# Two-layer kernel (cross attention, then a top-2 expert MLP): the gathered rows are transposed by SyncE's transposing DMAs instead of TensorE and ScalarE's copy

## The chip, the cores and the metric

One core of one Trainium2 chip. The metric is the device time of one launch in microseconds (us). The kernel before takes 813.24 us, the median of 3 runs (811.27 to 814.58). Its profiled execution is a run of its own and took 818.82 us; the span of its trace is 817.0 us.

## The reference, cut to what matters

`x` and `ctx` are 64 batches of 128 rows of 256 numbers, all float32.

```
# layer 1: x = x + xattn(layernorm(x), ctx, ctx)
score = softmax(einsum('bci,bcj->bij', ctx, q) / 16, axis=0)     # softmax over the 64 batches
out   = einsum('bci,bij->bcj', ctx, score)
# layer 2: x = x + moe(layernorm(x)); 8192 tokens of 256, 8 experts, hidden 512, top 2
logits = x @ router_w.T ; topk = top_k(logits, 2) ; probs = softmax(topk)
hmid   = gelu(x @ w1[e].T + b1[e])            # 256 -> 512, per chosen expert
y      = hmid @ w2[e].T + b2[e]               # 512 -> 256
out    = sum over the two chosen experts of probs * y
```

## The kernel before, in words

The first three stages read `ctx` and `x` three times: scores and their maximum over the batches, exponentials and their sum, and then attention with the routing logits (`attend`). They end near 300 us of the span. `attend` leaves for each token one row in a DRAM table (`rows_first`), 514 words wide: the layer's result x2 (256 float32 words), the normalised row as a high and a low float16 half, that is 512 float16 numbers in the next 256 words (from `XN`), and the two probabilities. Short routing work then sorts the tokens by expert: for each of two rounds (first choice, second choice) 39 groups of 256 tokens, each group owned by one expert. That makes `ALL` = 78 groups.

The expert stage runs from 331 us to the end, one group a step, as a software pipeline written out by hand: in each step every engine runs the parts of `group` in the order of its source, each part for another group, `L_...` steps after the group's gather.

- GpSimd (POOL), L517 to L532: in step g it issues the two indirect DMAs that gather the 256 rows of group g into two of the 12 row buffers (6 lanes of two, L506), then waits until the group of 4 steps ago is summed (`x_sum`) and issues the two indirect DMAs that scatter it (L513), to `rows_second` in round one, to the output in round two. Between the rounds, for 4 groups, x2 is gathered once more from `rows_second` (`late_loads`) after the scatters of round one have landed.
- TensorE, L661 to L695: the first product of group g-3 (24 matmuls of 256 columns, L670), then the transposes of group g-2 (8 of 128x128 float16 into PSUM bank 0, L681), then the second product of group g-4 (24 matmuls of 256 columns, L693). The wait of the first product for the transposed rows is L664, the wait of the transposes for the gathered rows is L676, and L677 holds them until the bank is copied out.
- ScalarE, L1044 to L1059: four Gelus of group g-3 (L1051), then the copy of the transposed rows of group g-2 from PSUM to `xT`, one of two buffers in SBUF (L1059).
- VectorE, L935 to L960: splits the Gelu's result in a high and a low float16 half (L942, L944), adds the bias (L931), and adds probability times product to the row (L958), which raises `x_sum`.
- SyncE (SP) has nothing to do in this stage: its last transfer, `b2` at L434, is issued before the routing.

The row buffers are read by the transposes and freed by the landing of the scatter (`x_out`, six semaphores, one a lane). A late gather overwrites the row buffer that the transposes read, so it waits for them (L525).

Of the kernel before, what the change touches and what calls it, by code (L numbers as in the profile page):

```python
# [26 lines left out]
F16 = mybir.dt.float16  # L27
# [3 lines left out]
ACT = mybir.ActivationFunctionType  # L31
AX_X = mybir.AxisListType.X

P = 128
BATCH, ROWS, DIM = 64, 128, 256
EXPERTS, HID = 8, 512
TOKENS = BATCH * ROWS
HC = DIM // P
FC = HID // P
GROUP = 256  # L40
SUB = GROUP // P
# [8 lines left out]
XN = DIM  # L50
# [4 lines left out]
PAIRS = BATCH // 2  # L55
RING = 4
LANES = 6
L_TR, L_G1, L_G2 = 2, 3, 4


def pipeline(eng, count, unroll, peel, last_lag, body):
# [41 lines left out]
def live(i, k, lag, count):  # L103

    return not isinstance(i, int) or 0 <= i + k - lag < count


def after(eng, sem, count):

    if not isinstance(count, int) or count > 0:  # L110
        eng.wait_ge(sem, count)
# [21 lines left out]
def xattn_ffn(nc, x, ctx, router_w, w1, b1, w2, b2, out):  # L133
# [7 lines left out]
    with ExitStack() as stack:  # L141
        def sb(name, shape, dt=F32):
            return stack.enter_context(nc.sbuf_tensor(name, shape, dt))

        def sem(name):
            return stack.enter_context(nc.semaphore(name))

        def sems(name, n):
            return [sem(f"{name}{i}") for i in range(n)]
# [4 lines left out]
        w1T = [sb(f"w1T_{p}", [P, FC, HC, EXPERTS * P], F16) for p in ("high", "low")]  # L154
# [15 lines left out]
        ident16 = sb("ident16", [P, P], F16)  # L170
# [22 lines left out]
        psum = stack.enter_context(nc.psum_tensor("psum", [P, 8, 512], F32))  # L193
# [63 lines left out]
        a_logit = sem("a_logit")  # L257
# [29 lines left out]
        def take(words, rows=P):  # L287
            taken[0] += words
            return slots[0:rows, taken[0] - words:taken[0]]
# [33 lines left out]
        row_buf = [take(ROW) for _ in range(LANES * SUB)]  # L323
# [2 lines left out]

        flat = work[:].rearrange("p a b -> p (a b)")
        act32 = [flat[:, j * FC * GROUP:(j + 1) * FC * GROUP] for j in range(2)]
        xT = [flat[:, 2 * FC * GROUP + j * 512:2 * FC * GROUP + (j + 1) * 512].bitcast(F16) for j in range(2)]


        x_rows_in = sems("x_rows_in", LANES)
        x_late_in = sems("x_late_in", L_G2)
        x_out = sems("x_out", LANES)
        x_tr = sem("x_tr")
        x_xT = sem("x_xT")
        x_hid = sem("x_hid")
        x_act = sem("x_act")
        x_high = sem("x_high")
# [4 lines left out]
        ALL = ROUNDS * GROUPS  # L344
# [11 lines left out]
        def late_loads(step):  # L356

            first = step - L_G2 + (step > GROUPS + L_G2)
            return [g for g in range(first, step - L_G2 + 2) if is_late(g) and step >= GROUPS + L_G2]
# [74 lines left out]
            sp.dma_start(b2_all, b2.rearrange("e (o h) -> o (e h)", o=1).to_broadcast([P, EXPERTS * DIM])).then_inc(r_b2, 16)  # L434


        @block.gpsimd
        def _(pool):
            pool.memset(ident[:], 0.0).then_inc(s_zero, 1)
# [63 lines left out]
            def gather(sources, g, signal):  # L503

                for s in range(SUB):
                    pool.indirect_dma_start(row_buf[g % LANES * SUB + s], None, sources,  # L506
                                            bass.IndirectOffsetOnAxis(ap=index[:, g * 4 + s:g * 4 + s + 1], axis=0)).then_inc(signal, 16)
# [9 lines left out]
            for step in range(ALL + L_G2):  # L517
                if step == GROUPS:
                    pool.wait_ge(r_index, 2)
                if step == GROUPS + L_G2:  # L520
                    for r in range(LANES):
                        pool.wait_ge(x_out[r], 32 * len(range(r, GROUPS, LANES)))
                for g in late_loads(step):
                    pool.wait_ge(x_rows_in[g % LANES], 32 * len(range(g % LANES, g + 1, LANES)))
                    pool.wait_ge(x_tr, g + 1)  # L525
                    gather(table[1], g, x_late_in[g - GROUPS])
                if step < ALL:
                    after(pool, x_out[step % LANES], step // LANES * 32)
                    gather(table[0] if step < GROUPS or is_late(step) else table[1], step, x_rows_in[step % LANES])
                if step >= L_G2:  # L530
                    pool.wait_ge(x_sum, step - L_G2 + 1)
                    scatter(step - L_G2)  # L532
# [5 lines left out]
        def _(pe):  # L538
            pe.wait_ge(s_const, 1)
            pe.wait_ge(s_rw_in, 16)  # L540
            for h in range(HC):
                mm = pe.transpose(psum[:, 6, h * 8:h * 8 + 8], rw_in[:, h * P:(h + 1) * P], ident[0:8, 0:8])
            pe.wait_ge(s_b1_in, 16)
            for f in range(FC):
                mm = pe.transpose(psum[:, 7, f * 8:f * 8 + 8], work[0:EXPERTS, 16 + f // 2, (f % 2) * P:(f % 2 + 1) * P], ident[0:8, 0:8])
# [87 lines left out]
            for r in range(ROUNDS):  # L633

                pe.matmul(psum[:, r, :], before[:], onehot[:, r * 512:(r + 1) * 512], start=True, stop=False)
                for e in range(EXPERTS):
                    mm = pe.matmul(psum[0:BATCH, 2, r * 8 + e:r * 8 + e + 1], hot[:, r, :, e], ones16[:, 0:1], start=True, stop=True)
# [21 lines left out]

            def group(i, k, n, rnd):  # L660
                if live(i, k, L_G1, ALL):  # L661
                    g, r2 = i + k - L_G1, (k - L_G1) % 2
                    e = pe.value_load(owner_i[0:1, bass.ds(g, 1)], min_val=0, max_val=EXPERTS - 1)
                    pe.wait_ge(x_xT, g + 1)  # L664
                    after(pe, x_act, g * 2 - 2)
                    for f in range(FC):
                        h = psum[:, 2 + 2 * r2 + f // 2, (f % 2) * GROUP:(f % 2 + 1) * GROUP]
                        for c in range(HC):
                            for px, pw in ((0, 0), (1, 0), (0, 1)):
                                mm = pe.matmul(h, w1T[pw][:, f, c, bass.ds(e * P, P)], xT[r2][:, (px * HC + c) * GROUP:(px * HC + c + 1) * GROUP],  # L670
                                               start=(c == 0 and px == 0 and pw == 0), stop=(c == HC - 1 and pw == 1))
                        if f % 2:
                            mm.then_inc(x_hid, 1)
                if live(i, k, L_TR, ALL):
                    g, r = i + k - L_TR, (k - L_TR) % LANES
                    pe.wait_ge(x_rows_in[r], n * 32 + (k - L_TR) // LANES * 32 + 32)  # L676
                    after(pe, x_xT, g)  # L677
                    bank = psum[:, 0, :].bitcast(F16)
                    for c in range(2 * HC):
                        for s in range(SUB):  # L680
                            mm = pe.transpose(bank[:, (c * SUB + s) * P:(c * SUB + s + 1) * P],  # L681
                                              row_buf[r * SUB + s][:, XN:XN + DIM].bitcast(F16)[:, c * P:(c + 1) * P], ident16[:])
                    mm.then_inc(x_tr, 1)
                if live(i, k, L_G2, ALL):
                    g, r2 = i + k - L_G2, (k - L_G2) % 2
                    e = pe.value_load(owner_i[0:1, bass.ds(g, 1)], min_val=0, max_val=EXPERTS - 1)
                    pe.wait_ge(x_low, g * 2 + 2)
                    after(pe, x_sum, g - 1)
                    for s in range(SUB):
                        y = psum[:, 6 + r2, s * DIM:(s + 1) * DIM]  # L690
                        for f in range(FC):
                            for pa, pw in ((0, 0), (1, 0), (0, 1)):
                                mm = pe.matmul(y, act16[r2][pa][:, f * GROUP + s * P:f * GROUP + (s + 1) * P],  # L693
                                               w2T[pw][:, f, bass.ds(e * DIM, DIM)], start=(f == 0 and pa == 0 and pw == 0), stop=(f == FC - 1 and pw == 1))
                    mm.then_inc(x_y, 1)  # L695
                if is_step(i, k, LIST_STEP):
                    list_tokens(1)
# [278 lines left out]
        def _(act):  # L976
# [66 lines left out]
            def group(i, k, n, rnd):  # L1043
                if live(i, k, L_G1, ALL):  # L1044
                    g, r, r2 = i + k - L_G1, (k - L_G1) % LANES, (k - L_G1) % 2
                    e = act.value_load(owner_i[0:1, bass.ds(g, 1)], min_val=0, max_val=EXPERTS - 1)
                    after(act, x_low, g * 2 - 2)
                    for f in range(FC):
                        if f % 2 == 0:
                            act.wait_ge(x_hid, g * 2 + f // 2 + 1)  # L1050
                        last = act.activation(act32[r2][:, f * GROUP:(f + 1) * GROUP], psum[:, 2 + 2 * r2 + f // 2, (f % 2) * GROUP:(f % 2 + 1) * GROUP],  # L1051
                                              ACT.Gelu, bias=b1_rows[:, bass.ds(e * FC + f, 1)], scale=1.0 / WSCALE)
                        if f % 2:
                            last.then_inc(x_act, 1)
                if live(i, k, L_TR, ALL):
                    g, r2 = i + k - L_TR, (k - L_TR) % 2
                    act.wait_ge(x_tr, g + 1)
                    after(act, x_hid, g * 2 - 2)
                    act.activation(xT[r2], psum[:, 0, :].bitcast(F16), ACT.Copy).then_inc(x_xT, 1)  # L1059
            expert_steps(act, group)  # L1060


# [17 lines left out]
```

## Time and profile before

| what | value |
|---|---|
| median of 3 runs | 813.24 us |
| profiled execution, and the span of its trace | 818.82 us, 817.0 us |
| first gather of the expert stage issued at | 331.2 us of the span |
| first and last transposes on TensorE | 336.8 and 797.6 us |
| matmuls of the first and of the second product | 1872 and 1872 |
| transposes, their busy time | 624, 48.2 us |
| ScalarE's copies, their busy time | 78, 79.9 us |
| GpSimd's indirect DMAs | 164 gathers, 156 scatters |
| granted TensorE clock, mean of the span | 0.943 |

The table says how much there is of each kind. The matmul records are pipelined: one of 276 ns starts every 109 ns. So a step's length is read from the starts, and the share of the span that a kind of work costs from where it stands on the chain that ends last, not from its busy time. Times below are us from the start of the span unless said otherwise; clock 1.00 is the 2.4 GHz level.

### The profile page before, as it was taken

Reading aid. Unit: us, or ns where it says so; the run is one execution under the profiler, and the core shown is the slowest. Engines: PE = TensorE matmul, PEld = TensorE weight load, DVE = VectorE, ACT = ScalarE, POOL = GpSimd, SP = SyncE. Lnnn points to the kernel's source line nnn. Section 1 sums busy time; section 2 is a strip of 40 time slices with the busy share of each in tenths; the row PEclk is TensorE's granted clock in tenths of the full one; section 3 lists DMA queues with packets and bytes.
Section 4 is the critical chain, followed back from the end, with each engine's and each line's share of the span. In section 5 each row is a group of like instructions: output and inputs, shape, how many; then the busy total and the mean of one; then the engine's idle time right before and its main releaser. Section 6 shows DMA issues by size and latency. Waiting matters only on the chain. (4 is left out here: it accounts for less than half of the span.)

```text
span 817.0 us, 22178 instructions
## 1 busy us (share of the span) xinstructions
PE 742.1 (91%) x5931; PEld 647.5 (79%) x5932; DVE 618.5 (76%) x1520; ACT 387.1 (47%) x716; POOL 538.5 (66%) x658
## 2 busy tenths in 40 slices
PE   6999999598999844499999999999979999999995
PEld 4777888477788734399999999999958999999995
DVE  5998999897999967786667676627467766767664
ACT  3554666375766751144444445414424444444441
POOL 4664777586888720657777777736677777777764
PEclk9999999798999955599999999979999999999998
DMA  7887876256888650445555555534355444444440
GB/s 217 259 258 233 242 234 203 88 172 207 268 270 270 228 199 0 103 141 159 183 163 186 167 181 179 160 114 132 104 167 143 152 146 134 132 139 130 139 113 1
DMA packets 82201, 137.20 MB, mean 168 GB/s; under 512 B 10075, under 2 KB 55140, under 8 KB 82032
## 3 DMA queue, kind: packets, MB, share of 16 engines
q0 software_dynamic: 23104, 68.43, 28.0%
q1 hardware_dynamic: 59056, 68.26, 26.8%
q8 instruction: 22, 0.36, 0.2%
q14 instruction: 19, 0.16, 0.1%
HBM read 94.56 MB, written 47.59 MB: 174 GB/s over the span
## 5 line engine op out<-in xcount | busy, mean ns | idle before, releaser
L1051 ACT ACTIVATE work<-psum,b1T 128x256 f32<-128x256 f32 x312 | 131.0, 471 | 259.3 <-PE psum L670 259.2
L670 PE MATMUL psum<-work,w1T_high 128*128 128x256 f16 x1248 | 213.1, 276 | 2.7 <-ACT work L1059 2.7
L693 PE MATMUL psum<-w2T_high,slots 128*128 x1248 | 210.2, 274 | 1.1 <-issue 1.1
L670 PE MATMUL psum<-work,w1T_low 128*128 128x256 f16 x624 | 172.3, 276 | 0.0
L693 PE MATMUL psum<-w2T_low,slots 128*128 x624 | 170.8, 274 | 0.0
L942 DVE CAST slots<-work 128x512 f16<-128x512 f32 x156 | 68.8, 441 | 118.6 <-ACT work L1051 118.4
L670 PEld LDWEIGHTS psum<-work,w1T_high 128*128 x1248 | 123.4, 99 | 18.7 <-issue 3.1
L693 PEld LDWEIGHTS psum<-w2T_high,slots 128*128 128x128 f16 x1248 | 119.2, 98 | 14.8 <-issue 1.8
L551 PE MATMUL psum<-slots,work 128*128 (+1 forms) x512 | 124.2, 393 | 7.1 <-ACT slots L981 6.5
L506 POOL DMA_INDIRECT slots<-rows_first,slots x86 | 89.4, 1039 | 60.5 <-DVE slots L903 34.6
L513 POOL DMA_INDIRECT rows_second<-slots x78 | 83.4, 1069 | 55.9 <-issue 34.7
L551 PEld LDWEIGHTS psum<-slots,work 128*128 128x128 f32 x512 | 94.6, 193 | 31.8 <-issue 14.9
L944 DVE TENSOR_TENSOR slots<-work,slots 128x512 f16<-128x512 f32 x156 | 108.5, 696 | 5.4
L513 POOL DMA_INDIRECT out_x<-slots x78 | 81.9, 1050 | 42.4 <-issue 32.4
L1059 ACT ACTIVATE work<-psum 128x1024 f16<-128x1024 f16 x78 | 79.9, 1024 | 33.5 <-PE psum L681 33.5
L506 POOL DMA_INDIRECT slots<-rows_second,slots x78 | 77.5, 994 | 25.5 <-issue 25.2
L931 DVE SCALAR_TENSOR_TENSOR slots<-slots 128x256 f32<-128x256 f32 x156 | 68.7, 482 | 28.1 <-issue 13.9
L623 PE MATMUL psum<-slots,work 128*128 (+1 forms) x256 | 66.5, 404 | 4.4 <-DVE slots L822 4.3
L958 DVE SCALAR_TENSOR_TENSOR slots<-psum,slots 128x256 f32<-128x256 f32 x156 | 68.2, 479 | 2.8 <-PE psum L693 2.5
L670 PEld LDWEIGHTS psum<-work,w1T_low 128*128 x624 | 61.8, 99 | 7.9
L693 PEld LDWEIGHTS psum<-w2T_low,slots 128*128 128x128 f16 x624 | 61.3, 98 | 7.3
L478 POOL TENSOR_TENSOR smax<-slots,smax 128x768 f32<-128x768 f32 x31 | 52.3, 1686 | 19.1 <-ACT slots L988 17.4
(123 smaller groups left out, 1076.9 us busy)
## 6 DMA issues: line engine op xcount, KB each, us to landing
work<-in_ctx SPq DMA_DIRECT2D x96, 256.0 KB, 3.6
rows_first<-slots SPq DMA_DIRECT2D x32, 514.0 KB, 3.9
slots<-in_x SPq DMA_DIRECT2D x32, 256.0 KB, 3.8
work<-in_L_ffn_w SPq DMA_DIRECT2D x32, 256.0 KB, 3.2
work<-in_x SPq DMA_DIRECT2D x32, 256.0 KB, 3.1
slots<-rows_first,slots POOLq DMA_INDIRECT x86
rows_second<-slots POOLq DMA_INDIRECT x78
slots<-rows_second,slots POOLq DMA_INDIRECT x78, 3.7
```

The source lines that it names most:

```text
L506: pool.indirect_dma_start(row_buf[g % LANES * SUB + s], None, sources, bass.IndirectOffsetOnAxis(ap=index[:, g * 4 + s:g * 4 + s + 1], axi ...
L513: pool.indirect_dma_start(table[1] if g < GROUPS else out_rows, bass.IndirectOffsetOnAxis(ap=index[:, g * 4 + 2 + s:g * 4 + 3 + s], axis=0 ...
L551: mm = pe.matmul(psum[:, r2, h * DIM:(h + 1) * DIM], ctx_ring[:, place, h * P:(h + 1) * P], slot(b, 0, DIM), start=True, stop=True)
L623: mm = pe.matmul(psum[:, 2 + r, j * DIM:(j + 1) * DIM], a_ctxT[:, 2 * r + j, h * P:(h + 1) * P], slot(m * 2 + j, h * DIM, DIM), start=(h = ...
L670: mm = pe.matmul(h, w1T[pw][:, f, c, bass.ds(e * P, P)], xT[r2][:, (px * HC + c) * GROUP:(px * HC + c + 1) * GROUP], start=(c == 0 and px ...
L693: mm = pe.matmul(y, act16[r2][pa][:, f * GROUP + s * P:f * GROUP + (s + 1) * P], w2T[pw][:, f, bass.ds(e * DIM, DIM)], start=(f == 0 and p ...
L931: last = dve.scalar_tensor_tensor(rows[:, X2:X2 + DIM], b2_all[:, bass.ds(e * DIM, DIM)], rows[:, PR + now:PR + now + 1], rows[:, X2:X2 + ...
L942: dve.tensor_copy(act16[r2][0][:, cols], act32[r2][:, cols]).then_inc(x_high, 1)
L944: dve.tensor_tensor(act16[r2][1][:, cols], act32[r2][:, cols], act16[r2][0][:, cols], ALU.subtract).then_inc(x_low, 1)
L958: last = dve.scalar_tensor_tensor(rows[:, X2:X2 + DIM], psum[:, 6 + r2, s * DIM:(s + 1) * DIM], rows[:, PR + now:PR + now + 1], rows[:, X2 ...
L1051: last = act.activation(act32[r2][:, f * GROUP:(f + 1) * GROUP], psum[:, 2 + 2 * r2 + f // 2, (f % 2) * GROUP:(f % 2 + 1) * GROUP], ACT.Ge ...
L1059: act.activation(xT[r2], psum[:, 0, :].bitcast(F16), ACT.Copy).then_inc(x_xT, 1)
```

## The change

The eight TensorE transposes of a group and ScalarE's copy are removed. In their place SyncE issues, for each group, two transposing DMAs from SBUF to SBUF, one for each row buffer: 128 partitions x 512 float16 numbers in, `[128, 4, 128]` out. `xT` gets a third buffer. The first product waits for 32 counts on its buffer's semaphore; SyncE waits for the gathered rows and for the first product of three groups ago, which is the last reader of the buffer. The late gather waits on the DMAs' semaphore instead of on TensorE's. The lags of the other parts stay (3 and 4 steps).

```diff
-L_TR, L_G1, L_G2 = 2, 3, 4
+L_G1, L_G2 = 3, 4
+XT_RING = 3
...
-        xT = [flat[:, 2 * FC * GROUP + j * 512:2 * FC * GROUP + (j + 1) * 512].bitcast(F16) for j in range(2)]
+        xT = [flat[:, 2 * FC * GROUP + j * 512:2 * FC * GROUP + (j + 1) * 512].bitcast(F16) for j in range(XT_RING)]
...
+            sp.wait_ge(a_logit, PAIRS)
+            for g in range(ALL):
+                sp.wait_ge(x_rows_in[g % LANES], 32 * (g // LANES + 1))
+                after(sp, x_hid, 2 * (g - XT_RING + 1))
+                for s in range(SUB):
+                    sp.dma_start_transpose(xT[g % XT_RING].rearrange("p (c t) -> p c t", t=GROUP)[:, :, s * P:(s + 1) * P],
+                                           row_buf[g % LANES * SUB + s][:, XN:XN + DIM].bitcast(F16)).then_inc(x_xT[g % XT_RING], 16)
...
-                    pool.wait_ge(x_tr, g + 1)
+                    pool.wait_ge(x_xT[g % XT_RING], 32 * (g // XT_RING + 1))
...
-                    pe.wait_ge(x_xT, g + 1)
+                    pe.wait_ge(x_xT[rx], n * (32 * LANES // XT_RING) + ((k - L_G1) // XT_RING + 1) * 32)
...
-                if live(i, k, L_TR, ALL):
-                    g, r = i + k - L_TR, (k - L_TR) % LANES
-                    pe.wait_ge(x_rows_in[r], n * 32 + (k - L_TR) // LANES * 32 + 32)
-                    after(pe, x_xT, g)
-                    bank = psum[:, 0, :].bitcast(F16)
-                    for c in range(2 * HC):
-                        for s in range(SUB):
-                            mm = pe.transpose(bank[:, (c * SUB + s) * P:(c * SUB + s + 1) * P],
-                                              row_buf[r * SUB + s][:, XN:XN + DIM].bitcast(F16)[:, c * P:(c + 1) * P], ident16[:])
-                    mm.then_inc(x_tr, 1)
...
-                if live(i, k, L_TR, ALL):
-                    g, r2 = i + k - L_TR, (k - L_TR) % 2
-                    act.wait_ge(x_tr, g + 1)
-                    after(act, x_hid, g * 2 - 2)
-                    act.activation(xT[r2], psum[:, 0, :].bitcast(F16), ACT.Copy).then_inc(x_xT, 1)
```

What this moves on TensorE, in one step of the expert stage. Before, from the end of a first product (L670) over the transposes to the start of the second product (L693):

```order
L670 MATMUL psum<-work,w1T_low 128x256
L681 MATMUL psum<-ident,slots 128x128 [waits x_xT,x_rows_in5]
L681 MATMUL psum<-ident,slots 128x128 x7
L686 TENSOR_LOAD slots
L686 ISA x2
L687 REGISTER_ALU
L693 ISA [waits x_sum,x_low]
L693 MATMUL psum<-w2T_high,slots 128x256 x2
```

The same place after, where the first product is L679 and the second L692:

```order
L679 MATMUL psum<-work,w1T_low 128x256
L685 TENSOR_LOAD slots
L685 ISA x2
L686 REGISTER_ALU
L692 ISA [waits x_sum,x_low]
L692 MATMUL psum<-w2T_high,slots 128x256 x2
```

The eight transposes are gone, and with them TensorE's only wait for gathered rows. The wait for transposed rows stays at the head of the first product.

On SyncE, after the transfer of `b2`, the program ended before. After, it goes on with the transposes; these are the rows of three groups from the middle of it, and there are 156 such DMAs:

```order
L442 DMA_TRANSPOSE work<-slots 128x4x128 [waits x_hid,x_rows_in0]
L442 DMA_TRANSPOSE work<-slots 128x4x128
L442 DMA_TRANSPOSE work<-slots 128x4x128 [waits x_hid,x_rows_in1]
L442 DMA_TRANSPOSE work<-slots 128x4x128
L442 DMA_TRANSPOSE work<-slots 128x4x128 [waits x_hid,x_rows_in2]
L442 DMA_TRANSPOSE work<-slots 128x4x128
```

Nothing stands between them: a group's transposes are queued behind those of the groups before it and behind nothing else.

## Rows read from the trace of the kernel before

**Rows 1.** The page's busy times of the engines, share of the span, instructions.

```profile
PE 742.1 (91%) x5931; PEld 647.5 (79%) x5932; DVE 618.5 (76%) x1520; ACT 387.1 (47%) x716; POOL 538.5 (66%) x658
```

**Rows 2.** Windows, one in each round: busy us by engine, clock, DMA share, GB/s.

```profile
450.00:500.00 50.00, 50.00 (x496) 45.23 (x494) 34.25 (x70) 23.33 (x45) 36.23 (x36) 1.00 0.56 177
...
650.00:700.00 50.00, 50.00 (x492) 45.19 (x490) 34.68 (x71) 22.64 (x45) 35.95 (x37) 1.00 0.48 140
```

**Rows 3.** The chain that ended last, one step: start, length, what.

```profile
774.68 0.45 PE psum L681 x8
775.13 2.62 PE psum L693 x24
777.75 2.62 PE psum L670 x24
780.37 0.45 PE psum L681 x8
```

**Rows 4.** Waits in the expert stage: total us, times, longest.

```profile
ACT work L1051 <- PE psum L670: 259.2, 155, 14.8
...
POOL rows_second L513 <- DVE slots L958: 21.3, 3, 13.4
...
POOL out_x L513 <- DVE slots L958: 10.0, 4, 3.7
```

**Rows 5.** Timeline of TensorE at the stage's start: start, length, line, idle before.

```profile
336.83 1.01 PE L681 MATMUL psum<-ident,slots 128*128 128x128 f16 x8 [9.03 <-DMA slots<-rows_first,slots]
339.10 0.61 PE L670 MATMUL psum<-work,w1T_high 128*128 128x256 f16 x2 [1.26 <-ACT work L1059]
```

**Rows 6.** Timeline of GpSimd in round two, four DMAs issued without a wait.

```profile
644.02 1.02 POOL L513 DMA_INDIRECT out_x<-slots  x1 [0.30 <-issue]
645.34 1.00 POOL L513 DMA_INDIRECT out_x<-slots  x1 [0.30 <-issue]
646.64 1.00 POOL L506 DMA_INDIRECT slots<-rows_second,slots  x1 [0.30 <-issue]
647.94 0.98 POOL L506 DMA_INDIRECT slots<-rows_second,slots  x1 [0.30 <-issue]
649.23 1.02 POOL L513 DMA_INDIRECT out_x<-slots  x1 [0.30 <-issue]
```

**Rows 7.** Timeline of GpSimd in round one, from scatter to scatter.

```profile
371.17 1.04 POOL L513 DMA_INDIRECT rows_second<-slots  x1 [0.57 <-issue]
...
376.86 1.04 POOL L513 DMA_INDIRECT rows_second<-slots  x1 [0.58 <-issue]
```

**Rows 8.** The chain between two rounds: start, length, what.

```profile
584.85 1.00 DMA rows_second<-slots
589.16 3.44 DMA slots<-rows_second,slots
...
600.37 3.71 DMA slots<-rows_second,slots
...
610.96 3.70 DMA slots<-rows_second,slots
```

**Rows 9.** The chain in round two: a second product's start, a first product's start.

```profile
661.40 2.62 PE psum L693 x24
...
681.08 2.62 PE psum L670 x24
```

**Rows 10.** Timeline of GpSimd in round two, the last gather of one group.

```profile
669.97 0.98 POOL L506 DMA_INDIRECT slots<-rows_second,slots  x1 [0.30 <-issue]
```

**Rows 11.** The gathers' line L506: from issue to landing.

```profile
DMA to landing us min/median/max: 3.3/3.7/4.1
```

**Rows 12.** SyncE's 256 KB loads of L415: issue in ns, landing in us.

```profile
L415 SPq DMA_DIRECT2D work<-in_ctx x32: 368/373/470, 146.5 to 271.6; - x32
...
DMA to landing us min/median/max: 2.8/3.6/6.6
```

**Rows 13.** The page's DMA queues: packets, MB, share of 16 engines over the span.

```profile
q0 software_dynamic: 23104, 68.43, 28.0%
q1 hardware_dynamic: 59056, 68.26, 26.8%
```

**Rows 14.** Timeline of TensorE behind a gap between the rounds.

```profile
606.76 0.62 PE L681 MATMUL psum<-ident,slots 128*128 128x128 f16 x8 [2.37 <-DMA slots<-rows_second,slots]
...
610.60 0.42 PE L693 MATMUL psum<-w2T_low,slots 128*128 x1
...
611.09 0.27 PE L693 MATMUL psum<-w2T_low,slots 128*128 x1
```

More of the change, by code:

```diff
@@ L334, in xattn_ffn @@
         x_out = sems("x_out", LANES)
-        x_tr = sem("x_tr")
-        x_xT = sem("x_xT")
+        x_xT = sems("x_xT", XT_RING)
         x_hid = sem("x_hid")
@@ L661, in group @@
                 if live(i, k, L_G1, ALL):
-                    g, r2 = i + k - L_G1, (k - L_G1) % 2
+                    g, r2, rx = i + k - L_G1, (k - L_G1) % 2, (k - L_G1) % XT_RING
                     e = pe.value_load(owner_i[0:1, bass.ds(g, 1)], min_val=0, max_val=EXPERTS - 1)
-                    pe.wait_ge(x_xT, g + 1)
+                    pe.wait_ge(x_xT[rx], n * (32 * LANES // XT_RING) + ((k - L_G1) // XT_RING + 1) * 32)
                     after(pe, x_act, g * 2 - 2)
@@ L669, in group @@
                             for px, pw in ((0, 0), (1, 0), (0, 1)):
-                                mm = pe.matmul(h, w1T[pw][:, f, c, bass.ds(e * P, P)], xT[r2][:, (px * HC + c) * GROUP:(px * HC + c + 1) * GROUP],
+                                mm = pe.matmul(h, w1T[pw][:, f, c, bass.ds(e * P, P)], xT[rx][:, (px * HC + c) * GROUP:(px * HC + c + 1) * GROUP],
                                                start=(c == 0 and px == 0 and pw == 0), stop=(c == HC - 1 and pw == 1))
```

## The prediction

> **What bounds the kernel now.** I read the page's busy times first: TensorE is busy 91% of the span, more than any other engine [rows 1]. That is an average over stages, so next come windows of the stage that the change touches. In both rounds of the expert stage TensorE is busy 50.00 of 50.00 us at clock 1.00, while GpSimd has 36 us and the DMA engines a share of 0.56 in round one and 0.48 in round two [rows 2]. Then the chain that ended last. The reader is to see its period: transposes 0.45 us, second product 2.62, first product 2.62, and again, 780.37 - 774.68 = 5.69 us a step, all of it TensorE [rows 3]. The waits confirm it: ScalarE waits 259 us for the first product, and the expert loop's GpSimd waits for VectorE only 31.3 us in 7 places [rows 4].
>
> GpSimd is a close second, though, and its busy time hides that. Between two of its DMA instructions lie 0.30 us that are not counted as busy. In round two four instructions that wait for nothing take 649.23 - 644.02 = 5.21 us [rows 6]. In round one a step is 5.69 us with an idle time of 0.57 in it where 0.30 is the least, so its own work takes 5.69 - 0.27 = 5.42 us [rows 7]. So GpSimd, which must issue four DMAs a step, can run at most 0.27 to 0.48 us a step faster than now.
>
> **The change part by part.**
>
> The transposes leave TensorE. On the chain they are 0.45 us a step [rows 3], so at most 78 x 0.45 = 35 us, and TensorE's step becomes 2 x 2.62 = 5.24 us. GpSimd needs 5.42 in round one and 5.21 in round two. The step is the longer of the two: 5.42 in round one (gain 0.27) and 5.24 in round two (gain 0.45). The 5.42 holds one scatter that took 0.17 us longer than its neighbours, and I take that as partly an accident of phase: the middle, 0.33, for round one, and 0.42 for round two, since no engine pair runs at its bound without some slip.
>
> How many steps gain? Not the ones between the rounds: from 584.85 to the landing at 610.96 + 3.70 = 614.66 the chain runs over GpSimd's DMAs and their landings [rows 8]. These 30 us are about five of TensorE's steps and stay. Two or three more steps at the start stand in a filling pipeline. I count 36 steps in round one and 35 in round two: 36 x 0.33 + 35 x 0.42 = 11.9 + 14.7 = 27 us.
>
> ScalarE's copy of 1.02 us goes as well. ScalarE waits for TensorE 259 us in this stage [rows 4], so the copy lies beside other work and costs nothing but for the first groups: the first product starts 2.27 us after the first rows are there, 1.01 for the transposes and 1.26 for the copy [rows 5]. After, it waits for SyncE's DMAs. With their latency L (next paragraph) of 4 us that is 1.7 us lost once. The 1.3 us or so that the second first product waited for its copy come back, so I enter nothing.
>
> The DMAs. Two questions: latency and rate. For latency, what counts is how long the rows lie ready before the first product wants them. In round two a second product ends at 661.40 + 2.62 = 664.02 [rows 9]. Its sum lets GpSimd scatter and then gather the group that is first multiplied at 681.08, three steps later [rows 9]. The last gather of that group is issued at 669.97 and takes 0.98 [rows 10], and lands 3.7 us after that [rows 11], at 674.65. So the loop from the product's end to the landing is 10.6 us, and there are 681.08 - 674.65 = 6.4 us for the transposes. With a step of 5.24 the loop closes in 15.7 us and leaves 5.1 us. No transposing DMA is in the trace. The nearest rows are SyncE's loads of 256 KB, the bytes of one group: issue 0.37 us and landing 3.6 us after it, 2.8 at best and 6.6 at worst [rows 12]. I take L = 0.37 + 3.6 = 4.0 us, under 5.1, so nothing is late. The ends are 3.2 us (hidden) and 0.37 + 6.6 = 7.0 us, where the loop of three steps would take 17.6 us, 5.87 a step.
>
> For rate, the two DMAs of a group must be through in a step, or they pile up in SyncE's queue whatever the slack. Bytes say yes: a group adds 256 KB, and the engines move 177 GB/s at share 0.56 [rows 2], 316 GB/s at full share, so 0.8 us of engine time; they are busy 0.56 x 5.69 = 3.2 us a step in round one and 2.7 in round two, and 4.0 fits into 5.24. Packets may say no. Rows of a 128 x 128 block are 256 bytes, 2 x 128 x 4 = 1024 of them a group, 64 for each of 16 engines. SyncE's packets took 0.268 x 16 x 817 us / 59056 = 59 ns each [rows 13], at 1.2 KB a packet. If one of 256 bytes costs as much, that is 64 x 59 = 3.8 us, and the step becomes 3.2 + 3.8 = 7.0 us in round one and 6.5 in round two. The other end of this bound is the price by bytes. I take the price by bytes, because the trace's two queues have nearly one price by bytes (59 ns for 1.16 KB, and 0.280 x 16 x 817 us / 23104 = 158 ns for 2.96 KB [rows 13]), so a fixed part doesn't show in them.
>
> The Trainium skill speaks on both sides here. Its page Advanced Engine Details and Errata, section X-Bar Transpose (TRN2), says that transposing DMAs are as fast as regular ones, some 350 to 400 GB/s; by it a group is an estimated 0.7 us and nothing changes in the sum. Its page VectorE: DVE Perf Modes, section The three transpose paths, gives 1309 ns for a 128x128 block by DMA and says to use TensorE for such a block where PSUM will do. Taken eight times in turn that is an estimated 10.5 us a step, about 1180 us in all. No row of this trace tells which of them holds for eight blocks at a time, out of SBUF and beside gathers.
>
> SyncE's new waits have nothing queued behind them but later transposes. The wait for the first product of three groups ago is over long before: that product ended two steps before the rows land. The third buffer costs nothing. GpSimd's late gathers wait for transposes of groups gathered a lane's round before, while the chain there is its own landings [rows 8]; should L be 7 us, it loses a few us once.
>
> Sum: 818.8 - 27 = 792 us for the profiled execution. That execution stood 5.6 us above the median of the runs, so I forecast 813.2 - 27 = 786, and enter 787 for the gathers' and scatters' somewhat later landings.
>
> **The rivals.**
>
> A, the forecast: the transposes hide, and TensorE and GpSimd share the bound. 776 (35 us saved, and 2 us of TensorE's waits for rows with it) to 800 (GpSimd's 5.42 in both rounds and some slips: 71 x 0.2 = 14 us saved). Chance 0.47.
>
> B, a wait takes the place of the work removed: L between 5.1 and 7.0 us. The loop then sets 5.3 to 5.87 a step. At 5.87 it is 71 x 0.18 = 13 us slower than before, 826; at 5.3 it is 28 us better. Most of this lies in 800 to 826. For it: landings up to 6.6 us where the DMA engines were loaded. Against it: in this stage they are less loaded. Chance 0.13.
>
> C, packets: the DMA engines become the bound. Steps of 7.0 and 6.5 us, on average 6.75, that is 75 x 1.06 = 80 us more, 893. The slower case as one mechanism with a place and a point: SyncE's queue on the 16 engines, and it decides as soon as a 256-byte packet costs more than (5.69 - 3.2) / 64 = 39 ns in round one. In between it gives 830 to 930. For it: pieces four times smaller than any here. Against it: the price by bytes. Chance 0.17.
>
> D, the crossbar takes one transfer after another, each for its whole latency: 2 x (0.37 + 3.6) = 7.9 us a step, 75 x 2.2 = 166 us more, 979. If instead each of the eight blocks were such a transfer, at the least landing of 2.8 us [rows 12], a step would take 22 us and the kernel over 2000 us: the outer end. The skill's 1309 ns would stand between the two. For it: nothing in the trace; against it: GpSimd's DMAs overlap, one issued every 1.3 us [rows 6] where one takes 3.7 to land [rows 11]. Chance 0.23, for 930 and above.
>
> In C and D TensorE idles 1 to 3 us each step. After 2.37 us of idle the trace shows it at half the clock, 0.42 us for a matmul of 0.27, until about 610.8 [rows 14]. That costs 1.6 us, 5.24 + 1.6 = 6.8 us of work a step, which still fits under 6.75 to 7.9, so I add nothing. That the change doesn't do what it says I don't count as a case: TensorE's instructions are gone.
>
> **How the numbers follow.** The time is A's, 787; A's own range is 776 to 800. Below 776 I leave 0.04. To leave out no more than 0.2 in all the range must reach through B and C and to D's first price: up to 980, with 0.14 above. About 0.5% (4 us) is what a measurement can tell from no change. Faster (under 809): A, and 0.04 of B, 0.51. Same (809 to 817): 0.06, of B and the edge of C. Slower: the rest, 0.43.
>
> **What would show it.** Right: the step between two first products on the chain near 5.3 us, no idle time of TensorE before the first product's line L679, GpSimd's idle time before its scatters down to 0.30 us, and the first product at the start about 2 us later than before. GpSimd's lines would take a larger share of the chain. B would show as short waits of L679 for SyncE's DMAs at an unchanged DMA share; C as a DMA share near 1 with many packets under 512 bytes and landings of gathers well above 3.7 us; D as waits of L679 with a low DMA share, and SyncE's DMAs landing one after the other at an even distance. I am wrong if that distance, for two of them, is over 5.7 us.

## The result, and the profile after

The changed kernel takes 834.21 us (median of 4 runs, 829.51 to 839.5) against 813.33: ratio 1.025, 95% interval 1.022 to 1.029. Slower by 21 us, where the forecast was 787 us. Its profiled execution took 832.83 us, its span is 831.0 us.

The page of the changed kernel: busy times, then DMA queues (packets, MB, share of 16 engines), as in [rows 1, 13].

```profile
PE 720.0 (87%) x5307; PEld 604.4 (73%) x5308; DVE 618.6 (74%) x1520; ACT 315.3 (38%) x638; POOL 537.7 (65%) x658
...
q1 hardware_dynamic: 143920, 88.73, 39.3%
q0 software_dynamic: 23104, 68.43, 32.4%
```

TensorE's and ScalarE's work did go (624 matmuls, 78 activations). The share of the busiest engine fell from 91% to 87% although the span grew: a sign that the bound is no longer an engine. SyncE's queue has 84,864 packets more, 544 for each of the 156 transposing DMAs.

Windows of the changed kernel, columns as in [rows 2]:

```profile
450.00:500.00 50.00, 48.25 (x427) 40.38 (x424) 34.85 (x71) 15.12 (x36) 35.44 (x36) 1.00 0.90 218
...
700.00:750.00 50.00, 47.93 (x425) 40.33 (x422) 35.05 (x69) 15.12 (x36) 35.42 (x36) 1.00 0.78 180
```

In these two windows TensorE's busy time is some 2 us short of 50, at the full clock, and GpSimd does no more in 50 us than before. 425 matmuls in 50 us stand where 495 stood; 56 of the old ones made a step and 48 of the new, so that both kernels do 8.8 steps in 50 us. Here the changed kernel gains nothing and loses nothing. Busy shares alone hide what the waits show; this is the changed kernel's expert stage (total us, times, longest), to be read beside [rows 4]:

```profile
ACT work L1050 <- PE psum L679: 379.2, 155, 34.1
...
PE psum L679 <- DMA work<-slots: 49.4, 31, 13.1
POOL rows_second L522 <- DVE slots L957: 37.5, 10, 14.1
...
POOL out_x L522 <- DVE slots L957: 20.1, 12, 3.7
```

TensorE waits 49 us for the transposing DMAs, in 31 of 78 steps, and GpSimd 58 us for sums where it waited 31. The parties wait for each other in a ring. In round two the chain of the changed kernel goes round it seven times, with stretches between in which TensorE's or GpSimd's own work is all that it holds. One time round (start, length, what):

```profile
710.67 5.54 DMA slots<-rows_second,slots
716.23 1.19 SPq L442
...
717.46 5.12 DMA work<-slots
722.58 0.23 issue
722.81 1.50 PE psum L679 x12
...
728.22 0.44 DVE slots L930
...
729.05 0.87 DVE slots L957 x2
...
730.77 1.02 POOL out_x L522
...
732.09 1.00 POOL out_x L522
...
733.39 1.00 POOL slots L515
...
734.70 0.71 POOL slots L515
```

Each `DMA` row runs from the start of a DMA's issue to its landing. Read the chain from the last gather of one group (710.67) to the last gather of the group four later (734.70): 5.5 us to the landing; 6.6 us from there to the first product (722.81); 7.1 us through Gelu, VectorE's halves, bias and the sum (729.92); then two scatters and two gathers on GpSimd. 24.0 us for four steps, 6.0 a step. GpSimd's scatters in about the same stretch:

```profile
701.05 1.02 POOL L522 DMA_INDIRECT out_x<-slots  x1 [0.75 <-issue]
...
712.98 1.14 POOL L522 DMA_INDIRECT out_x<-slots  x1 [1.18 <-DVE slots L957]
...
724.74 1.02 POOL L522 DMA_INDIRECT out_x<-slots  x1 [1.19 <-DVE slots L957]
```

Four steps lie between the first and the last row: 23.69 / 4 = 5.92 against 5.69 before. That is a slow stretch and no mean of the stage. The starts of first products in TensorE's timeline tell where the time went. These are the 11th, 34th, 49th and 78th of the changed kernel:

```profile
403.98 0.38 PE L679 MATMUL psum<-work,w1T_high 128*128 128x256 f16 x2
...
535.51 0.38 PE L679 MATMUL psum<-work,w1T_high 128*128 128x256 f16 x2
...
648.07 0.39 PE L679 MATMUL psum<-work,w1T_high 128*128 128x256 f16 x2 [0.67 <-DMA work<-slots]
...
814.20 0.38 PE L679 MATMUL psum<-work,w1T_high 128*128 128x256 f16 x2
```

The same four in the kernel before:

```profile
397.62 0.38 PE L670 MATMUL psum<-work,w1T_high 128*128 128x256 f16 x2
...
528.41 0.38 PE L670 MATMUL psum<-work,w1T_high 128*128 128x256 f16 x2
...
635.42 0.38 PE L670 MATMUL psum<-work,w1T_high 128*128 128x256 f16 x2
...
800.33 0.38 PE L670 MATMUL psum<-work,w1T_high 128*128 128x256 f16 x2
```

| stretch, by first products | before | after | more |
|---|---|---|---|
| first gather's issue to the 11th | 66.40 us | 79.26 us | 12.9 us |
| 11th to 34th, round one | 130.79, 5.69 a step | 131.53, 5.72 a step | 0.7 |
| 34th to 49th, between the rounds | 107.01 | 112.56 | 5.6 |
| 49th to 78th, round two | 164.91, 5.69 a step | 166.13, 5.73 a step | 1.2 |

From the first gather (324.72) to the end the changed kernel takes 506.3 us, the one before 817.0 - 331.22 = 485.8, so 20.5 us more in all. In the middle of both rounds it keeps the old pace. It misses there the 0.45 us a step that TensorE no longer works, and the loss against the kernel before is made at the start and between the rounds. Of the 12.9 us the first product had 1.8, and from the 5th group to the 11th a step takes 6.8 us.

A part of it is TensorE's clock. Both kernels have some 10 us at half the clock near 540 us, which makes no difference. Apart from that, TensorE went back to it once before the change, between the rounds, for 3.4 us [rows 14]. In the changed kernel the first products that begin at 344.90, 397.07 and 620.88, after 5.24, 2.20 and 7.06 us of idle time, show 0.42 us for a matmul of 0.27. The last of them on the chain:

```profile
620.88 5.31 PE psum L679 x24
```

It takes 5.31 us where 2.62 is the rule [rows 3]. The three take some 6 us more than at the full clock, the one place before 1.6, so I put the clock at 5 of the 20.5 us, an estimate.

### The profile page after: what moved, and what is told of

Same layout as the page of the kernel before. It is cut to its first block and busy times, and to the rows that moved or that the text cites. A ratio compares the mean times of both kernels' runs of the same rounds, so it can differ in the third digit from the quotient of the medians.

```text
span 831.0 us, 20879 instructions
## 1 busy us (share of the span) xinstructions
PE 720.0 (87%) x5307; PEld 604.4 (73%) x5308; DVE 618.6 (74%) x1520; ACT 315.3 (38%) x638; POOL 537.7 (65%) x658
## 5 line engine op out<-in xcount | busy, mean ns | idle before, releaser
L679 PE MATMUL psum<-work,w1T_high 128*128 128x256 f16 x1248 | 218.9, 281 | 49.8 <-DMA work<-slots 49.4
L692 PE MATMUL psum<-w2T_high,slots 128*128 x1248 | 209.1, 273 | 7.1 <-issue 4.1
L679 PEld LDWEIGHTS psum<-work,w1T_high 128*128 x1248 | 121.7, 100 | 77.5 <-issue 60.6
L679 PE MATMUL psum<-work,w1T_low 128*128 128x256 f16 x624 | 174.8, 280 | 0.0
L692 PE MATMUL psum<-w2T_low,slots 128*128 x624 | 170.1, 273 | 0.0
L692 PEld LDWEIGHTS psum<-w2T_high,slots 128*128 128x128 f16 x1248 | 118.1, 98 | 33.1 <-issue 19.6
L522 POOL DMA_INDIRECT rows_second<-slots x78 | 81.5, 1045 | 69.5 <-DVE slots L957 37.5
L560 PEld LDWEIGHTS psum<-slots,work 128*128 128x128 f32 x512 | 93.9, 192 | 31.6 <-issue 15.0
L515 POOL DMA_INDIRECT slots<-rows_second,slots x78 | 79.3, 1017 | 25.7 <-issue 25.1
L679 PEld LDWEIGHTS psum<-work,w1T_low 128*128 x624 | 62.9, 101 | 8.8
L692 PEld LDWEIGHTS psum<-w2T_low,slots 128*128 128x128 f16 x624 | 61.1, 98 | 7.1
L632 PEld LDWEIGHTS psum<-slots,work 128*128 128x128 f32 x256 | 47.9, 197 | 10.2 <-issue 4.6
```

The costliest lines, as they stand in the source:

```text
L522: pool.indirect_dma_start(table[1] if g < GROUPS else out_rows, bass.IndirectOffsetOnAxis(ap=index[:, g * 4 + 2 + s:g * 4 + 3 + s], axis=0 ...
L560: mm = pe.matmul(psum[:, r2, h * DIM:(h + 1) * DIM], ctx_ring[:, place, h * P:(h + 1) * P], slot(b, 0, DIM), start=True, stop=True)
L632: mm = pe.matmul(psum[:, 2 + r, j * DIM:(j + 1) * DIM], a_ctxT[:, 2 * r + j, h * P:(h + 1) * P], slot(m * 2 + j, h * DIM, DIM), start=(h = ...
L679: mm = pe.matmul(h, w1T[pw][:, f, c, bass.ds(e * P, P)], xT[rx][:, (px * HC + c) * GROUP:(px * HC + c + 1) * GROUP], start=(c == 0 and px ...
```

## The experiments

The theory: a loop of latencies sets the step wherever it is longer than the engines' own work: GpSimd's gather, its landing, SyncE's two issues, the transposes' landing, first product, Gelu, sum, and back to GpSimd. No engine and no bandwidth is full; the loop has four steps to close in. The rivals: contention (the transposes load the DMA engines and slow everything), the DMAs' own rate, and that GpSimd would have eaten the gain anyway. Ratios are to the kernel before, run on the same chip.

**No transposes.** SyncE's loop is gone, and the first product reads a constant tile, so the output is not the layer's. The first product still waits for its group's rows.

```diff
-            for g in range(ALL):
-                sp.wait_ge(x_rows_in[g % LANES], 32 * (g // LANES + 1))
...
-                    pe.wait_ge(x_xT[rx], n * (32 * LANES // XT_RING) + ((k - L_G1) // XT_RING + 1) * 32)
+                    pe.wait_ge(x_rows_in[(k - L_G1) % LANES], n * 32 + (k - L_G1) // LANES * 32 + 32)
```

> The changed kernel without any transposes: SyncE's DMAs are left out, and every first product multiplies one constant tile (computed once), but still waits for its group's gathered rows. So this is the change with a transpose that costs nothing, and its output is not the layer's. Theory 1 (a loop of latencies: sum of a group on VectorE, scatter and gather issued by GpSimd, landing of the gather, the two transposing DMAs, first product; four steps long, 23.7 us in the changed kernel's trace, 5.92 us a step): without the transposes and with gathers landing in 3.7 us the loop is 15.3 us, 3.8 a step, so TensorE (5.24) and GpSimd (5.2 to 5.4) bound, as my forecast had it: 783 to 793 us, ratio to before 0.963 to 0.975. Rival (GpSimd or something else was the bound all the time and the removed TensorE work was never worth anything): over 805 us, ratio over 0.99.

Measured: 782.85 us, ratio 0.961 (0.957 to 0.965). The removed work was worth 31 us, a little more than my 27. GpSimd did not eat it: in round one too its step is 5.23 and 5.24 us in this kernel (scatters at 425.40, 430.63, 435.87), not 5.42. Its timeline in round two of this kernel:

```profile
705.83 1.02 POOL L516 DMA_INDIRECT out_x<-slots  x1 [0.30 <-issue]
707.14 1.02 POOL L516 DMA_INDIRECT out_x<-slots  x1 [0.30 <-issue]
708.48 1.00 POOL L509 DMA_INDIRECT slots<-rows_second,slots  x1 [0.30 <-issue]
709.78 0.98 POOL L509 DMA_INDIRECT slots<-rows_second,slots  x1 [0.30 <-issue]
711.07 1.02 POOL L516 DMA_INDIRECT out_x<-slots  x1 [0.30 <-issue]
```

711.07 - 705.83 = 5.24 us, TensorE's step, with no idle time above 0.30: here both are full, as forecast. The rival that the work was worth nothing falls.

**Transposes run, unread.** The same, but SyncE's DMAs run, with waits that keep them in order; GpSimd too waits for a lane's transposes before it gathers into the lane again (not shown).

```diff
+                if g >= XT_RING:
+                    sp.wait_ge(x_xT[g % XT_RING], 32 * (g // XT_RING))
                 for s in range(SUB):
                     sp.dma_start_transpose(...)
...
-    ... xT[rx][:, (px * HC + c) * GROUP:(px * HC + c + 1) * GROUP],
+    ... xC[:, (px * HC + c) * GROUP:(px * HC + c + 1) * GROUP],
```

> The transposing DMAs run as in the changed kernel, but nobody on TensorE waits for them: the first product multiplies a constant tile and waits for the gathered rows alone (the output is not the layer's). Theory 1 (latency in the loop): the loop loses the 6.6 us from the rows' landing to the first product and keeps gathers that land in 5.5 us instead of 3.7: 17.1 us, 4.3 a step, not binding; 785 to 797 us, ratio 0.965 to 0.98. Theory 2 (contention: the transposes load the DMA engines and slow everything else, GpSimd's DMAs first): near the changed kernel, 822 to 836 us, ratio 1.01 to 1.03. In both, gathers land later than 3.7 us.

Measured: 784.93 us, ratio 0.963 (0.961 to 0.965). All 156 DMAs are in flight and the kernel is as fast as without them. One window of this kernel in round one, one in round two:

```profile
440.00:490.00 50.00, 50.00 (x459) 44.52 (x458) 37.09 (x77) 16.56 (x40) 38.30 (x39) 1.00 0.98 238
680.00:730.00 50.00, 49.88 (x458) 44.44 (x456) 38.43 (x76) 16.03 (x39) 38.42 (x39) 1.00 0.85 195
```

A DMA share of 0.98, and TensorE at 50.00 of 50.00. So between this kernel and the changed one (49 us) lies, but for the waits named, only what the first product waits for. Contention as a cost of its own falls: it counts as far as it makes a landing in the loop later. Rate falls too: the transposes keep up with a step of 5.24 us.

**One step more between gather and product.**

```diff
-LANES = 6
-L_G1, L_G2 = 3, 4
-XT_RING = 3
+LANES = 8
+L_G1, L_G2 = 4, 5
+XT_RING = 4
...
-    resume = -(-(GROUPS + L_G2) // LANES)
+    resume = -(-(GROUPS + 2 * L_G2) // LANES)
```

> The changed kernel with one more step between gather and first product: lags 4 and 5 instead of 3 and 4, eight lanes of row buffers and four xT buffers, and the code between the rounds shifted to fit. It computes all of the layer. Theory 1 (latency): the loop has five steps for its 23.7 us, 4.7 a step, so TensorE and GpSimd bound: 785 to 800 us, ratio 0.965 to 0.985, a little more lost between the rounds because the pipeline is longer. Theory 2 (contention) or theory 3 (the transposing DMAs' own rate, 2.24 us each at the start where they stand back to back, 4.5 a group, and more beside gathers): 815 us or more, ratio over 1.0.

Measured: 798.49 us, ratio 0.980 (0.978 to 0.982): faster than the kernel before by 16 us. Repeated with 5 rounds on another chip it was 0.979 (0.976 to 0.983), with this expectation:

> The lag experiment once more, unchanged, beside the kernel with the two small edits on the same chip: ratio 0.978 to 0.983, 796 to 801 us.

The 2.24 us "back to back" in the first of these expectations were a misreading of mine, of this merged row of the changed kernel's SyncE timeline:

```profile
330.14 15.69 SPq L442 DMA_TRANSPOSE work<-slots  x7
```

Its 15.69 us hold the waits between the seven DMAs; each issue by itself took 1.19 to 1.32 us there. The rival of a limiting rate took its size from it.

The lag experiment runs the same DMAs for each group. Its 11th first product begins 66.2 us after the first gather (327.04 to 393.21), as before the change, and not 79.3. At this place its chain in round two is all TensorE, two products of 2.62 and nothing between, 5.24 us a step:

```profile
701.52 2.62 PE psum L679 x24
704.14 2.62 PE psum L692 x24
706.76 2.62 PE psum L679 x24
```

**Control: lanes and buffers alone.** `LANES = 8`, `XT_RING = 4`, lags 3 and 4.

> Control for the deeper pipeline: eight lanes and four xT buffers, but the lags 3 and 4 of the changed kernel. Theory 1: the loop doesn't go through a free lane or a free xT buffer, so nothing changes, 829 to 840 us, ratio 1.02 to 1.035. Rival (GpSimd waited for a lane's scatters to land, or SyncE for a free xT buffer): faster than 822 us.

Measured: 838.97 us, ratio 1.032 (1.028 to 1.035), the changed kernel or slightly worse. So room alone gives nothing; it is the lag that does.

**Half the blocks.** Each DMA transposes the high halves alone, two blocks of 128x128 for four. The low half of `xT` holds constants, so the output is not the layer's; TensorE works as before.

```diff
-    ... t=GROUP)[:, :, s * P:(s + 1) * P],
-        row_buf[g % LANES * SUB + s][:, XN:XN + DIM].bitcast(F16)).then_inc(x_xT[g % XT_RING], 16)
+    ... t=GROUP)[:, 0:HC, s * P:(s + 1) * P],
+        row_buf[g % LANES * SUB + s][:, XN:XN + P].bitcast(F16)).then_inc(x_xT[g % XT_RING], 16)
```

> The changed kernel with the low halves left untransposed: each transposing DMA takes 128x256 float16 instead of 128x512, two blocks for four, and the low half of xT holds values written once (the output is not the layer's; TensorE multiplies as before). It tells what the 6.6 us from landing to first product are made of. If SyncE's 1.25 us and the 5.1 us of landing go by blocks: about 0.65 and 3.3, and gathers land in about 4.6 us; the loop of 23.7 us loses 0.6 + 1.8 + 0.9 = 3.3 us, 5.1 us a step, so TensorE bounds: 785 to 800 us, ratio 0.965 to 0.985. If they are fixed costs of a DMA: the loop stays, 828 to 840 us, ratio over 1.015. In between: a mixture.

Measured: 813.32 us (10 runs), ratio 1.000 (0.998 to 1.003), in between. The chain of this kernel:

```profile
676.70 1.17 SPq L443
677.91 4.65 DMA work<-slots
```

SyncE's issue is 1.17 us, and from the second issue's start to the landing 4.65 where it was 5.12: 6.6 us became about 6.1. These are single places. Over the chains in round two the landing took 4.64 to 6.20 us with two blocks and 4.81 to 5.84 with four, so no clear share of it goes by size; the issue hardly at all (1.17 against 1.19). The other part of the gain I can't split: gathers on its chain landed in 3.8 to 4.6 us, in the changed kernel's in 4.2 to 5.7.

**Both at once.** The kernel before with SyncE's transposes added, written to buffers that nobody reads.

> The kernel before, whole, with the transposing DMAs added: SyncE transposes every group into buffers that nobody reads. Theory 1 (latency in the loop): gathers land 1.8 us later, but the transposes on TensorE have 3.4 us of slack in the kernel before, so 812 to 820 us, ratio 0.998 to 1.007. Theory 2 (contention is a cost of its own): ratio of 1.01 and more.

Measured: 817.1 us, ratio 1.004 (1.002 to 1.007). The DMA traffic by itself costs about 3 us, 5 at most, where the transposes are on TensorE.

**The deeper pipeline without the change.** The kernel before with `LANES = 8` and `L_TR, L_G1, L_G2 = 3, 4, 5`.

> The kernel before with the deeper pipeline of the lag experiment (eight lanes, lags 3, 4 and 5). TensorE bounds its steps already, so theory 1 gives nothing for it: 811 to 820 us, ratio 0.997 to 1.008, the upper part for the longer filling and the stretch between the rounds. If the deeper pipeline is a gain by itself, and not because it takes the transposing DMAs out of the loop: under 805 us.

Measured: 811.78 us, ratio 0.996 (0.994 to 0.999), 3 us faster, a little under the ratio that I gave. So 13 of the lag experiment's 16 us come from the change, freed of its wait.

**Bias behind the sum.** The lines of `add_bias` for group g-3 move on VectorE from ahead of the sum of group g-4 to behind it.

```diff
-                    if not is_late(g):
-                        add_bias(g, r, n * 32 + (k - L_G1) // LANES * 32 + 32, round_of(i, k, L_G1, rnd))
...
                     last.then_inc(x_sum, 1)
+                if live(i, k, L_G1, ALL) and not is_late(i + k - L_G1):
+                    add_bias(i + k - L_G1, ...)
```

> The changed kernel with one edit that has nothing to do with DMAs: VectorE adds the bias of group g-3 behind the sum of group g-4 instead of ahead of it. The bias additions take 0.88 us and stand in the loop as the trace shows it, right ahead of the sum for which GpSimd waits. Theory 1 (a loop of four steps of latencies bounds): it loses up to 0.88 us, or 0.65 where the second product's end becomes the later one, 0.16 to 0.22 us a step, over some 71 steps 11 to 16 us: 817 to 826 us, ratio 1.003 to 1.016. If TensorE, GpSimd or the DMA engines bound by their own work, nothing changes: 830 to 840 us, ratio 1.02 to 1.03.

Measured: 825.74 us, ratio 1.015 (1.011 to 1.018): 9 us less than the changed kernel, a little less than the 11 to 16 expected. Moving an addition on VectorE, an engine busy 70% in this stage, makes the kernel faster, as a latency loop would have it. In this kernel the sum waits for the second product in 70 of 78 steps (in 3 before this edit), so the product is now the later of the two:

```profile
DVE slots L955 <- PE psum L692: 49.6, 70, 1.3
```

**A semaphore for each gather.** SyncE waits for half a group and issues its first DMA while the second gather is on its way.

```diff
-                sp.wait_ge(x_rows_in[g % LANES], 32 * (g // LANES + 1))
...
                 for s in range(SUB):
+                    sp.wait_ge((x_rows_in, x_rows_2)[s][g % LANES], 16 * (g // LANES + 1))
```

> The changed kernel with a semaphore of its own for each of a group's two gathers, so SyncE issues the first transposing DMA when the first 128 rows have landed and not when all 256 have. GpSimd issues the two gathers 1.3 us apart, so the first issue on SyncE (1.19 us) moves ahead of the second landing. Theory 1: the loop of 23.7 us loses 1.2 us, 0.3 us a step, at most 21 us over 71 steps; the bias edit got two thirds of its like figure, so 812 to 824 us, ratio 0.998 to 1.013. If SyncE's issue is not in the loop (only the landing is): 830 to 840 us, ratio 1.02 to 1.03.

Measured: 812.23 us, ratio 0.998 (0.994 to 1.001): 23 us less than the changed kernel by the ratios, for an issue of 1.19 us taken out of the loop. Expected were at most 21, which counted steps of the middle alone.

**All three** (lag, bias, semaphores).

> The lag experiment with both small edits (bias behind the sum, a semaphore for each gather). Its steps are TensorE's 5.24 us already, so theory 1 leaves only the places where TensorE still waits for the transposes: the first groups and the stretch between the rounds, 1.2 to 2 us at each of two or three places. 2 to 6 us less than the lag experiment: 792 to 797 us, ratio 0.973 to 0.979. No difference to it would say that these places hang on GpSimd's gathers alone.

Measured: 796.98 us, the median of six runs of which one took 1462.66 us for a reason that is not known; without that run the median is 795.29 and the ratio 0.977 (0.973 to 0.981). The lag experiment beside it: 798.8, 0.979 (0.976 to 0.983). The intervals overlap: no difference shown. The waits of TensorE in this kernel, first its wait for transposes, then for VectorE's halves:

```profile
PE psum L681 <- DMA work<-slots: 16.9, 4, 12.6
...
PE psum L694 <- DVE slots L946: 11.0, 3, 6.1
```

and in the lag experiment:

```profile
PE psum L679 <- DMA work<-slots: 23.2, 5, 13.2
PE psum L692 <- DVE slots L943: 7.8, 3, 5.3
```

What TensorE waits less for transposes it waits more for VectorE, some 3 us apart in all. The lag experiment stays 16 us above the kernel without a transpose, whose like waits are:

```profile
PE psum L672 <- DMA slots<-rows_first,slots: 10.0, 2, 8.9
PE psum L685 <- DVE slots L937: 7.1, 2, 6.8
```

31.0 against 17.1 us, so 14 of the 16 us can stand in these waits (the longest in the filling of the pipeline); no run took them away.

## Why the prediction was wrong

The step that failed is "I take L = 0.37 + 3.6 = 4.0 us, under 5.1, so nothing is late". On the chain L is 6.6 us (6.2 to 7.3 over its seven times round). The slack that it was set against was wrong as well: the gathers' landing was held at 3.7 us, where 4.2 to 5.7 came out. The sizes, by its own terms:

- SyncE's issue. I took 0.37 us, once, from plain loads [rows 12]. The transposing DMA holds SyncE for a median of 1.25 us (1.19 at least, 2.35 at most), and a group has two: 1.19 + 0.04 + 1.28 = 2.5 us. By the split experiment hiding one issue gave back all that the change had lost, 23 us.

```profile
716.23 2.51 SPq L442 DMA_TRANSPOSE work<-slots  x2
```

- Landing. From the start of the second issue to the landing are 5.12 us (717.46 to 722.58), 3.8 of them after its end. The 3.6 us of [rows 12] count from the start of the issue, so they hold the 0.37 that I added once more. Like for like I had 3.2 us after the issue, and 0.6 were missing; the issue is the larger miss. For the very first group, when few other DMAs ran, all of L was 4.3 us (330.14 to 334.43), two issues in it. What it takes beyond that later, like the gathers' longer landing, goes with the load on the DMA engines. So contention is likely to be in the loop as latency; no run splits it off.
- The gather's landing. I held it at 3.7 us and put "later landings" down as 1 us in the sum. On the changed kernel's chain gathers take 5.54 us from the start of their issue, in other places 4.2 to 5.7; before they took 3.44 to 3.71 [rows 8]. Here my working had an error the other way: the 3.7 of [rows 11] counts from the start of the issue too, and I added the 0.98 us of the issue [rows 10]. The slack at old landings was thus nearer to 6.1 than 5.1 us, and still too little.
- The sum on VectorE. I let GpSimd start from the second product's end. The sum now stands behind the bias and the halves of the next group, some 0.7 us later than that end; the bias experiment gave 9 us by taking the bias away.

With these the path from a second product's end to the first product three steps on is 10.6 - 1.0 + 1.8 + 0.7 + 6.6 = 18.7 us. I divided such a path by three. But TensorE's own two products stand in front of it and don't stretch when TensorE waits, so the loop is 18.7 + 5.24 = 23.9 us over four steps, 6.0 a step, as on the chain (24.0). The same slip is in my "17.6 us, 5.87 a step": it comes to (17.6 + 5.24) / 4 = 5.71, about the pace before. That "5.87" fell on the slower side is luck.

Rival B, "a wait takes the place of the work removed", was the mechanism: waits of L679 for SyncE's DMAs. I gave it 0.13. Rightly worked out, its worst case was no change, because I took for both unknowns the good row and varied only one at a time. Its price was also wrong in place. It counted 71 steps that are slower by 0.18 us, where the steps in the middle are slower by 0.03 to 0.04, and 18 of the 20.5 us lie at the start and between the rounds. "These 30 us ... stay" failed for the same reason: there the landings are the chain, and it took 5.6 us more. And I considered TensorE's clock in C and D only; in the forecast it stood at nothing, where some 5 us came of it.

One sign of B came out otherwise: I expected it at an unchanged DMA share, and the share rose from 0.56 to 0.90 in round one. That was C's sign, and C was wrong: 84,864 packets more took 0.393 x 16 x 831 us less 0.268 x 16 x 817 us, 1722 us, 20 ns each. The other queue's packets, as many as before, took 648 us more; with them it is 28 ns. That is half of my dear price (59 ns), under the 39 ns from which C would decide, and the unread experiment runs at share 0.98 without its engines losing anything. A high share was no bound here. It adds up the times of packets, and these can overlap: a window of 50 us of the unread experiment reaches 1.02.

```profile
450.00:500.00 50.00, 50.00 (x460) 44.67 (x459) 37.16 (x78) 16.08 (x39) 38.41 (x39) 1.00 1.02 237
```

D is wrong too: the two DMAs of a group are issued 1.23 us apart (716.23 and 717.46 on the chain), and both have landed 6.35 us after the first issue's start, where one after the other, each for its 5.12 us, would take 10.2. So they overlap, and the unread experiment passes two of them every 5.24 us. That is half of the estimate of 10.5 us that I drew from the Trainium skill's 1309 ns a block (VectorE: DVE Perf Modes, The three transpose paths), at least for blocks that go four to a DMA. The other page's sentence, that transposing DMAs are as fast as regular ones (Advanced Engine Details and Errata, X-Bar Transpose (TRN2)), fits the landing roughly (3.8 us behind the issue, 3.2 for the plain load) and not the issue (1.25 against 0.37 us).

What was right: the 0.45 us of a step, worth 27 us by my count and 31 us measured without transposes, more mostly because GpSimd's own step in round one was 5.24 and not 5.42; that GpSimd would be full at the new step; and the very start: the first product came 9.7 us after the first gather's issue (324.72 to 334.43), 7.9 before, 1.8 us later where I had 1.7:

```profile
334.43 0.61 PE L679 MATMUL psum<-work,w1T_high 128*128 128x256 f16 x2 [13.13 <-DMA work<-slots]
```

The next ten groups lost 11 us more, of which I had nothing. That ScalarE's copy costs nothing no run shows by itself; the 31 us hold it.

## What to carry to other kernels

Work that is moved from a full engine to DMAs turns busy time into latency, so before moving it, draw the loop that the buffers and semaphores close, add its latencies with the bad row for each unknown, count the engines' own work that stands in it, and divide by the number of steps that it has. Then look at the start and at every place where the pipeline runs dry, for the loop costs most there. If it is tight, deepen the pipeline in the same edit: the change that cost 2.5% gained 2% with one step more of lag and eight lanes. A loop also tells where small edits pay: here an edit of about 1 us on VectorE or SyncE, neither of them full, was worth 9 or 23 us.

## What the runs showed of the hardware

- A transposing DMA of 128x512 float16, SBUF to SBUF, occupies SyncE for a median of 1.25 us, and about as long with two blocks of 128x128 as with four (1.17 and 1.19 us on the chains above). From the start of its issue it lands in 4.8 to 5.8 us on the changed kernel's chain. It makes 544 packets (84,864 / 156), at 20 to 28 ns each.
- For the first group, with few DMAs beside them, two of them were issued and had landed within 4.3 us; on the chain in round two it took 6.2 to 7.3.
- Gathers land later beside these DMAs: in 4.2 to 5.7 us on the chain of round two, where it was 3.44 to 3.71.
- The DMA share of a window can be 0.98 to 1.02 with no engine slower for it: TensorE kept its 5.24 us a step, GpSimd its four DMAs.
- After waits of 5.24, 2.20 and 7.06 us TensorE's matmuls of the changed kernel took 0.42 us for 0.27, half the clock, for a whole first product or most of it.
